# Graph attention on one core: the penalty of a dense chunk put between the counts of a later tile, its rows asked for ahead of the score row, and the last score row loaded only in the branch that uses it

## The reference

```
h = x @ W;  s1 = h @ a1;  s2 = h @ a2
e = leaky_relu(s1[:, None] + s2[None, :], 0.2)
e = where(adj > 0, e, -9e15)
out = layernorm(x + elu(softmax(e, axis=1) @ h))
```

## Time and profile before

| what | us |
|---|---|
| median of 3 runs (lowest, highest) | 887.17 (886.31, 889.92) |
| the profiled execution's own time | 888.37 |
| its span | 886.2 |
| busy in it: PE / DVE / ACT / POOL | 581.7 / 610.8 / 574.5 / 608.9 |
| transfers | 332.76 MB, mean 375 GB/s |

### The profile page before, as it was taken

How to read it: one execution, slowest core, us unless ns; L and a number is a source line. 1 busy time by engine, 2 the same in 40 slices (tenths; PEclk the granted TensorE clock), 3 DMA queues, 4 the chain that set the end, 5 groups by cost and what they waited for, 6 DMA issues and landing times. The chain is left out here.

```text
span 886.2 us, 10111 instructions
## 1 busy us (share of the span) xinstructions
PE 581.7 (66%) x2385; PEld 348.2 (39%) x2385; DVE 610.8 (69%) x2337; ACT 574.5 (65%) x531; POOL 608.9 (69%) x694
## 2 busy tenths in 40 slices
PE   6588985566883858757777277665766758487640
PEld 4466661232451424434434134342433424254330
DVE  4256652576996758779986577778679678487772
ACT  3035536767975968877777397575976949498410
POOL 4486426777788676788847768788777876667741
PEclk9799998877898878989889788878889879799755
DMA  8999998999999999999999889999999999899405
GB/s 332 397 405 403 377 373 329 404 407 392 403 414 417 418 415 413 415 417 416 415 417 379 345 341 417 418 351 401 381 418 420 413 397 400 339 413 409 153 23 219
DMA packets 65295, 332.76 MB, mean 375 GB/s; under 512 B 19558, under 2 KB 38215, under 8 KB 48720
## 3 DMA queue, kind: packets, MB, share of 16 engines
q1 hardware_dynamic: 36320, 289.68, 80.0%
q0 software_dynamic: 25456, 29.79, 10.1%
q10 hardware_dynamic: 3456, 12.58, 3.8%
HBM read 357.37 MB, written 17.14 MB: 423 GB/s over the span
## 5 line engine op out<-in xcount | busy, mean ns | idle before, releaser
L1453 POOL DMA_INDIRECT GATH<-haug,ids x448 | 474.8, 1060 | 130.4 <-issue 125.8
L1269 ACT ACTIVATE WORK<-ADJ 128x4096 bf16<-128x4096 int32 x128 | 461.7, 3608 | 121.1 <-PE pk L519 74.7
L519 PE MATMUL pk<-WORK,D 128*128 128x512 bf16 x1024 | 293.1, 439 | 204.4 <-ACT WORK L1269 204.0
L519 PEld LDWEIGHTS pk<-WORK,D 128*128 128x128 bf16 x1024 | 103.2, 108 | 374.5 <-ACT WORK L1269 250.2
L530 PE MATMUL acc<-GATH,diag 128*128 128x256 f32 x512 | 140.4, 423 | 45.8 <-DVE diag L808 45.6
L530 PEld LDWEIGHTS acc<-GATH,diag 128*128 128x128 f32 x512 | 106.5, 213 | 80.5 <-DVE diag L808 60.3
L1312 ACT ACTIVATE WORK<-WORK,smalls 128x1024 f32<-128x1024 int32 x16 | 18.4, 1147 | 104.1 <-DMA WORK<-in_adj_dram,smalls 71.6
L505 PE MATMUL acc<-Waug,GATH 128*128 128x258 f32 x256 | 66.1, 403 | 12.2 <-DVE GATH L735 12.2
L818 DVE SCALAR_TENSOR_TENSOR PART<-GATH,smalls,PART 128x256 f32<-128x256 f32 x128 | 62.1, 485 | 4.5
L802 DVE RECIPROCAL smalls<-smalls 128x1 f32<-128x1 f32 x64 | 10.1, 158 | 77.2 <-ACT smalls L1278 76.3
L505 PEld LDWEIGHTS acc<-Waug,GATH 128*128 128x128 f32 x256 | 48.9, 198 | 24.9 <-issue 17.0
(11 more groups left out here) (177 smaller groups left out, 715.5 us busy)
## 6 DMA issues: line engine op xcount, KB each, us to landing
ADJ<-in_adj_dram SPq DMA_DIRECT2D x128, 2048.0 KB, 13.9
haug<-GATH POOLq DMA_DIRECT2D x32, 258.0 KB, 8.4
WORK<-s_row ACTq DMA_DIRECT2D x16, 512.0 KB, 10.5
out_dram<-Y SPq DMA_DIRECT2D x32, 256.0 KB, 12.2
GATH<-haug,ids POOLq DMA_INDIRECT x448, 8.5
X<-in_x_dram SPq DMA_DIRECT2D x1, 4096.0 KB, 33.0
WORK<-in_adj_dram ACTq DMA_DIRECT2D x8, 512.0 KB, 13.7
WORK<-s_row SPq DMA_DIRECT2D x1, 4096.0 KB, 11.8
```

The lines of the kernel that those rows point to most:

```text
L519: done = nc.tensor.matmul(pk[s % PKS][:], D16[:, k, :], A16[:, q % 2, k * BW:(k + 1) * BW], start=(half == 0 and k == 0), stop=(half == 1 ...
L1269: act.activation(A16[:, q % 2, :], ADJ[:, q % 4, :], ACT.Relu, scale=HALF_SCALE if q % 2 else 1.0, accum_out=degree[:, q // 2, q % 2:q % 2 ...
L1453: pool.indirect_dma_start(out=GATH[:, r, k * DA:(k + 1) * DA], out_offset=None, in_=haug, in_offset=bass.IndirectOffsetOnAxis(ap=ids[:, t ...
```

## The change

Three edits:

1. `mid_penalise` of a chunk leaves the end of ACT's step c+1 and goes to step c+2, between the two counts of that step. So one more count stands ahead of it.
2. In `mid_load` the adjacency chunk (first round) is asked for ahead of the score row's chunk. Both are on ACT's queue.
3. The 4 MB load of `s2_all` leaves SP and goes to POOL, as the first thing inside the closing branch `If(n > 0)` of `rounds`. DVE's `mask_columns(0, ...)` moves behind the last step into one branch, and its wait for the load with it. SP no longer waits for `packed`, `extras_stored`, `mid_stored` and the load. `store` is defined some lines earlier, which changes only line numbers.

```diff
@@ SP
-            sp.wait_ge(packed, HALVES)
-            sp.wait_ge(extras_stored, 32)
-            sp.wait_ge(mid_stored, 32)
-            sp.dma_start(s2_all, s2_row.rearrange("t p -> (t p)").partition_broadcast(P)).then_inc(s2_loaded, 16)
-            sp.wait_ge(s2_loaded, 16)
             for b in range(2):
                 sp.wait_ge(out_stored[b], 16 * (G // 2))
@@ DVE
             for s in range(T, LAST + 1):
                 before_scan(s)
                 after_scan(s)
-                if s == LAST - 3:
-                    with dve.If(n > 0):
-                        dve.wait_ge(s2_loaded, 16)
-                        mask_columns(0, range(CH // 2))
-                if s == LAST - 2:
-                    with dve.If(n > 0):
-                        mask_columns(0, range(CH // 2, CH))
             with dve.If(n > 0):
+                dve.wait_ge(s2_loaded, 16)
+                mask_columns(0, range(CH))
                 row_maxima(0)
                 make_logits(0, [0])
@@ ACT, mid_load
-                act.dma_start(mid_s2, s2_row.rearrange("t p -> (t p)")[cols].partition_broadcast(P))\
-                    .then_inc(mid_s2_loaded, 16)
                 if x < MC:
                     if x >= 1:
                         act.wait_ge(mid_exped, x)
                     act.dma_start(mid_adj, adj_tiles[:, 0, cols]).then_inc(mid_adj_loaded[0], 16)
+                act.dma_start(mid_s2, s2_row.rearrange("t p -> (t p)")[cols].partition_broadcast(P))\
+                    .then_inc(mid_s2_loaded, 16)
@@ ACT, mid_pieces and the loop over steps
-                for x in chunk_at(s - 1):
-                    mid_penalise(x)
...
             for s in range(EARLY, LAST + 1):
                 if s < T:
                     count(2 * s)
+                for x in chunk_at(s - 2):
+                    mid_penalise(x)
+                if s < T:
                     count(2 * s + 1)
@@ POOL
-            rounds(pool, n, None, dense_round)
+            def load_s2():
+                pool.wait_ge(mid_stored, 32)
+                pool.dma_start(s2_all, s2_row.rearrange("t p -> (t p)").partition_broadcast(P)).then_inc(s2_loaded, 16)
+
+            rounds(pool, n, load_s2, dense_round)
```

More of the change, by code:

```diff
@@ L434, in load_half, with store @@
                 sp.dma_start(ADJ[:, q % 4, :], adj_tiles[:, q // 2, half:half + HW]).then_inc(adj_loaded[q % 4], 16)
+            def store(j):
+                sp.wait_ge(normed, 2 * (j + 1))
+                sp.dma_start(out_tiles[:, GROUP * j:GROUP * (j + 1), :], Y[:, j % 2, :, :])\
+                    .then_inc(out_stored[j % 2], 16)
             sp.dma_start(Waug[:, :, 0:D], W.rearrange("(c p) d -> p c d", p=P)).then_inc(params_loaded, 16)
@@ L445, in _ @@
             load_x(2)
[L446 to L449, removed]
             for q in range(4, HALVES):
```

## The result

| | us |
|---|---|
| before, median of 4 runs (lowest, highest) | 887.08 (886.31, 889.92) |
| after, median of 4 runs (lowest, highest) | 879.94 (878.55, 880.48) |
| ratio after / before, 95% interval | 0.9911 (0.9886 to 0.9936) |
| span of the profiled execution, before and after | 886.2, 877.6 |

The change made the kernel 7.1 us faster; the interval of the ratio allows 5.7 to 10.1. I had forecast 21 us, with a range of 859.5 to 878: the sign was right, the size was not.

A forecast was written before the change was run, and what follows sets the result against it. The prediction took the stream of adjacency halves at one DMA rate, plus its holes and the end, as the bound. 888.4 - 10.0 (end) - 11 (body) = 867.4; the median lies 1.2 lower: 866.2 us, range 859.5 to 878.

The forecast's parts named there:

- I take -10.0 us: At the kernel's end: dropping SP's score row load and its wait saves 10.0 us, between 9.5 and 10.5.
- the span ends within 0.5 us of POOL's last instruction: Sign expected in the new profile: nothing but POOL's last instruction ends the span, with no SP wait for the score row.
- I take 11: In the body: one more count ahead of the penalty wins 11 us, out of 0 to 15.6.
- POOL's two waits: POOL's waits for a chunk's exponent (7.8 us) and a tile's ids (11.1 us), forecast to fall from 18.9 to some 4.
- ACT's idle time isn't the price: the stream's holes are: In the body: the gain is counted from DMA windows below 416 GB/s, not from up to 28.8 us of ACT time.
- 15.6 us is the most that the stream can win: One more half queued during each stall closes every hole except the first, of which 2.1 us stay.
- my 17.7 us: Sum of the stream's holes in the listed windows, each priced by its rate's shortfall from 416 GB/s.
- My second account, POOL's 14.9 us: POOL's waits for exponents and ids in the loop with the stalls lose up to 3.6 us each, 14.9 together.
- (a): Rival, chance 0.30: the hole moves, chunk rows land later, only the end is gained: 877.2 us (872 to 878).
- (b): Rival, chance 0.12: the whole 15 us of both accounts, up to 4 more from smaller holes: 862 to 858 us.
- (c): Rival, chance 0.03: slower, the later penalty delays mask, normalisation, store and loads; 935 us at a full count per chunk.
- (d): Rival, chance 0.03 shared with a partial loss: n above 0, so the closing branch runs and loads the row anyway.

The follow-up runs named there:

- e1: Edit 3 alone (score row's load out of the end) on the kernel before: 882.92 us, ratio 0.9960.
- e2: Edit 1 alone (penalty behind one more count) on the kernel before: 882.42 us, ratio 0.9955.
- e6: The changed kernel without the 8 loads of the score row's chunks in the second round, for timing alone: 870.80 us, ratio 0.9834.
- e9: The kernel before with 6 instead of 7 indirect gathers for a tile, for timing alone: 879.66 us, ratio 0.9928.
- e10: Edit 1 on the kernel before with 6 gathers for a tile (e9), for timing alone: 878.89 us, ratio 0.9920.
- e3: Edit 2 alone (adjacency chunk asked for ahead of the score row's chunk) on the kernel before: 885.53 us, ratio 0.9990.
- e4: The changed kernel with POOL's last wait and instruction moved into the closing branch, SP waiting for `mid_stored` at the end: 876.43 us, ratio 0.9892.

## Why the prediction was wrong, by its own steps

**Edit 3, "I take -10.0 us, ends -9.5 and -10.5. It hides behind nothing: no engine works after 876.06."** This is the first step that failed. Measured alone it is 3.1 us (e1). I had shown that the load stood behind all work, but not that nothing else did: POOL's drain ran at the same time and would end 2.4 to 2.9 us before it. The row was in the trace of before. Busy time and the chain of waits leave out such instructions of a queue; a query for the line of the block's end (L58) shows them. My own sign, "the span ends within 0.5 us of POOL's last instruction", is refuted by 7.4 us.

**Edit 1, "I take 11".** This is the second: 3.6 us measured (e2). Each of the two steps cost the forecast about half of what it missed, 6.9 and 7.4 us. The mechanism was there, the 15 stalls shrank by 4.4 us on average (104.1 to 37.9 us in all), and POOL's two waits fell from 18.9 to 12.9 us (I had put 4). What failed is the account of the stream, "ACT's idle time isn't the price: the stream's holes are", with its "15.6 us is the most that the stream can win". Here are e1 (body of before) and e2 in the same windows: length, busy by engine, PEclk, DMA share, GB/s. First e1:

```profile
480.00:530.00 50.00, 28.88 (x109) 14.72 (x107) 33.27 (x134) 32.76 (x29) 36.48 (x43) 0.80 0.88 350
570.00:600.00 30.00, 20.22 (x72) 12.17 (x72) 22.29 (x83) 20.12 (x21) 23.86 (x28) 0.77 0.93 359
815.00:820.00 5.00, 2.19 (x6) 0.87 (x7) 2.04 (x6) 3.75 (x5) 3.91 (x6) 0.80 1.03 403
820.00:824.00 4.00, 1.50 (x4) 0.41 (x3) 3.71 (x16) 3.11 (x2) 3.09 (x4) 0.82 0.88 359
```

Then e2:

```profile
480.00:530.00 50.00, 27.32 (x105) 13.77 (x102) 36.34 (x142) 36.25 (x33) 39.92 (x46) 0.83 0.96 384
570.00:600.00 30.00, 19.46 (x82) 12.32 (x83) 24.34 (x93) 22.18 (x23) 24.17 (x27) 0.83 0.98 359
815.00:820.00 5.00, 3.74 (x10) 1.82 (x11) 3.81 (x13) 3.89 (x5) 3.99 (x4) 0.66 0.32 114
820.00:824.00 4.00, 3.52 (x18) 2.07 (x16) 3.64 (x21) 1.54 (x3) 2.86 (x5) 1.00 0.07 21
```

Three things can be read. The hole at chunk 8 closed much as I said: 350 to 384 GB/s over 50 us is (384 - 350) / 416 x 50 = 4.1 us, for the 5.0 that I had put. At chunk 10 the share of the DMA engines rose from 0.93 to 0.98 while the rate stayed at 359: GB/s below 416 is not idle time, and I had counted it as such. In the earlier trace rows four of the windows stand at shares of 0.95 to 0.97, and 4.8 of my 17.7 us come from them. And at the end, between 820 and 824 us, e2's DMA share is 0.07, about one engine of 16 (0.0625), while e1's engines still all work. Yet the last half counts as landed at

```profile
825.64 3.62 ACT L1259 ACTIVATE WORK<-ADJ 128x4096 bf16<-128x4096 int32 x1 [2.53 <-DMA ADJ<-in_adj_dram]
```

in e1 and at

```profile
823.77 3.62 ACT L1269 ACTIVATE WORK<-ADJ 128x4096 bf16<-128x4096 int32 x1 [2.46 <-DMA ADJ<-in_adj_dram]
```

in e2. Most DMA engines are done some 7 us earlier, as the forecast would have it; the last half waits for a straggler, and it gained only 1.9 us.

The trace shows the straggler at work. Between 818.35 and 823.32 us in e2 the only packets of over 2 KB are eight of 16 KB, each starting where the one before ends: 128 KB, a sixteenth of a half. And the semaphore of each half is raised 16 times by its transfer; ACT's count of the last half starts just behind the sixteenth (823.75 us in e2, 825.62 in e1). How far the sixteenth lands behind the fifteenth, taken from these records (median over the halves that land in the stretch, us), and the two times of the last half:

| | 400 to 500 us | 550 to 750 | from 800 on | last half, 15th and 16th |
|---|---|---|---|---|
| before | 5.3 | 0.6 | 0.5 | 828.90, 828.92 |
| e1 | 5.5 | 0.4 | 0.3 | 825.31, 825.62 |
| e2 | 6.1 | 2.8 | 6.4 | 818.17, 823.75 |
| after | 5.6 | 3.9 | 6.5 | 819.08, 824.50 |
| e6 | 5.9 | 3.8 | 0.3 | 813.98, 814.00 |
| e9 | 4.7 | 5.7 | 7.8 | 814.69, 821.27 |
| e10 | 5.9 | 8.2 | 7.6 | 812.85, 819.87 |

So one share comes some 5 to 6 us late in each of these kernels between 400 and 500 us, ahead of the first large hole. The holes of before were idle time of the many, in which the one behind caught up. The window at chunk 8 in the trace of before shows that too. Of the half that lands there the fifteenth share is in at 506.29 us and the sixteenth at 513.27, with one engine's worth of traffic between:

```profile
510.00:512.00 2.00, 0.16 (x1) 0.13 (x2) 0.58 (x4) 2.00 (x3) 1.60 (x4) 0.50 0.07 25
```

In e2 the holes are smaller, the fifteen finish 7.1 us sooner than in e1 and the sixteenth 1.9: the step from holes to time was wrong, because the mean over 16 engines has holes that the one that sets the landing has not. e6 fits as well. A sixteenth of 4.2 MB at a sixteenth of 416 GB/s is 10 us on each engine; the sixteenth came 10.5 us sooner than in the changed kernel, the fifteenth only 5.1.

Which engine it is, whether it is always the same one, and why it falls behind, is not shown. The Trainium skill ("DMA: Bandwidth & Descriptors", section "Latency and other measured facts") says that two of the 16 DMA engines, 7 and 15, are usually the slower ones in traces, and suspects the descriptor rings of POOL's transfers. No run here names the engine. That fewer POOL gathers move the last count forward (823.8 in e2, 819.9 in e10, for 0.35 MB less to move) agrees with it but does not prove it.

The rest of e2's gain is POOL's. The ids of tile 63 and the gate behind which its gathers start, in e1 and then in e2:

```profile
835.25 0.16 DVE L771 TENSOR_SCALAR pens<-smalls 128x6 f32<-128x6 f32 x1
...
838.70 0.18 POOL L1440 TENSOR_TENSOR smalls<-smalls 128x1 f32<-128x1 f32 x1
```

```profile
833.70 0.16 DVE L776 TENSOR_SCALAR pens<-smalls 128x6 f32<-128x6 f32 x1
...
833.88 0.19 POOL L1451 TENSOR_TENSOR smalls<-smalls 128x1 f32<-128x1 f32 x1
```

POOL's gate was 3.45 us behind the ids and is 0.18 behind now: 1.55 us of the stream plus 3.27 of POOL's lag are the 4.82 between the two gates. (The profiled execution of e1 is 0.7 us above its median and that of e2 0.9 below, so these rows show more than the 3.6 us of the medians.) This also fits e9, where edit 1 is worth nothing: with 84 us less to issue, POOL has no lag at the end that edit 1 could take away (ids at 831.43, gate at 831.61), and the straggler, 7.8 us behind without edit 1 and 7.6 with it, sets the rest. My second account, POOL's 14.9 us, went wrong with it: its waits for ids were counted as won, but they come back when the stream can't follow (11.1 us in 3 waits before, 9.8 in 4 after). Nor was POOL without pause in all of the windows, as I wrote: 5.18 and 2.19 us of 10 stand in two of them.

**Edit 2** was put at 0 and is 0.5 us, with 0 inside the interval (e3). Right, and for the reason given: the wait for the chunk became a wait for the stream.

**The rivals.** The time of 879.94 us lies in none of the cases that I gave a price, since all of them took the 10 us of the end. (a), that the hole moves and only the end is won, had the better picture of the body, but priced it with the same wrong end; its body gain of 0 to 5 us holds the 3.6. Its mechanism, a later landing of the chunk, is hardly seen: the median from issue to landing of the second round's chunks went from 13.1 to 13.8 us. (b), 15 us and more from the body, is out by e2. (c) did not happen: DVE's waits at the mask are 13.6 us in the changed kernel (16.8 in e2, 13.8 before; the rows name nothing that ended them). Nor did (d): the load is gone, and the kernel moves 328.56 MB instead of 332.76.

## What to carry to other kernels

Before the work behind the last instruction is priced, ask the trace for what the queues do there, drains among them: a transfer that ends last may be hiding something nearly as long. A dip of the DMA rate is a hole only as far as the DMA share dips too, and even then the transfer that all wait for ends with its slowest engine, which may have had no hole. Compare when the last of a transfer's semaphore increments comes with when the one before it comes. Where two edits free the same slack, their gains don't add: test one on top of the other before a sum is made.

## What the runs showed of the hardware

- POOL's drain at the end of its stream takes 7.27 us here, with 448 indirect gathers of neighbours behind it, 5.22 with 384 and 3.92 with 320. It ends 7.2 us behind POOL's last instruction with 448, also when the stores are still under way (e4). At the program's start, with no transfer issued yet, POOL's drain takes 0.17 us.
- In a saturated stream one sixteenth of each transfer can land well behind the rest: in the changed kernel by a median of 5.6 us between 400 and 500 us and of 6.5 at the end. It then outlasts the others by that: 0.07 of the engines busy, 21 GB/s, from 820 to 824 us in e2. Where the others run dry, it catches up: 0.6 us in the kernel before, after the hole at chunk 8.
- Moved ahead of the score row's chunk on the same queue, the adjacency chunk of 0.5 MB landed 10.6 us after its issue (median) instead of 13.7.
